# Two mixture layers on one core: the experts' output bias added on GpSimd from a table on all partitions instead of by a selector matmul

## What is computed

```python
h = gelu(einsum('bsh,bhi->bsi', x, Wi[e]) + bi[e])     # 256 -> 1024
o = einsum('bsi,bih->bsh', h, Wo[e]) + bo[e]           # 1024 -> 256, bo: 8 x 256
r = o + x
y = (r - mean(r)) * rsqrt(var(r) + 1e-12) * gamma[e] + beta[e]
```

## Time and profile before

| | before |
|---|---|
| median of 3 runs | 488.36 us (488.33 to 488.38) |
| profiled execution | 488.29 us |
| its span, first to last instruction | 486.5 us |
| mean granted TensorE clock | 0.98 |
| busy: PE, DVE, ACT, POOL | 458.1, 341.8, 362.3, 343.7 us |

### The profile page before, as it was taken

One profiled execution on the slowest core, in us unless ns is written; L12 is line 12 of the kernel. 1 busy time (PEld: TensorE's weight loads), 2 busy tenths in 40 slices (PEclk: granted clock), 3 DMA queues, 4 the chain that ended last, 5 costly groups with the idle time before them and its releaser, 6 DMA issues.

```text
span 486.5 us, 18826 instructions
## 1 busy us (share of the span) xinstructions
PE 458.1 (94%) x5724; PEld 423.3 (87%) x5725; DVE 341.8 (70%) x910; ACT 362.3 (74%) x1087; POOL 343.7 (71%) x567
## 2 busy tenths in 40 slices
PE   3599999999999999999999999999999999999972
PEld 2388999999999999999999999999999999888861
DVE  7677777777777777777777787777777766665352
ACT  2499777887777877778877788777787777776631
POOL 5043677887778877887778877887778877754565
PEclk9889999999999999999999999999999999999995
DMA  3924334333333343433433333333332222220001
GB/s 105 333 73 106 95 99 104 104 102 92 98 100 95 103 104 87 99 96 102 104 89 95 102 101 98 86 98 101 101 98 65 60 62 61 62 56 25 26 22 34
DMA packets 66806, 44.33 MB, mean 91 GB/s; under 512 B 41537, under 2 KB 58322, under 8 KB 66642
## 3 DMA queue, kind: packets, MB, share of 16 engines
q1 hardware_dynamic: 65744, 43.68, 33.4%
q10 hardware_dynamic: 1026, 0.21, 0.2%
HBM read 35.47 MB, written 8.39 MB: 90 GB/s over the span
## 4 chain that ended last, share of the span: by engine, by line
PE 89%; DVE 3%; issue 2%; POOL 2%; ACT 2%; DMA 0%; POOLq 0%; DVEq 0%
PE p_o L1019 12%; PE p_o L1017 12%; PE p_o L1018 12%; PE p_h L1006 12%; PE p_h L1008 11%; PE p_h L1007 11%; PE p_d L1029 7%; PE p_u L1043 6%; PE p_t L1051 3%; PE p_u L1039 2%; PE p_o L1117 1%; PE p_h L947 1%; DVE W L810 1%; ACT h L639 0%; ACT ctab L591 0%
## 5 line engine op out<-in xcount | busy, mean ns | idle before, releaser
L1006 PE MATMUL p_h<-x_hi,W 128*128 128x128 f16 (+1 forms) x1088 | 183.5, 217 | 3.3 <-issue 3.3
L1007 PE MATMUL p_h<-x_lo,W 128*128 128x128 f16 (+1 forms) x1088 | 183.3, 217 | 0.0
L1008 PE MATMUL p_h<-x_hi,W 128*128 128x128 f16 (+1 forms) x1088 | 183.3, 217 | 0.0
L639 ACT ACTIVATE h<-p_h,bi_tile 128x128 f32<-128x128 f32 (+1 forms) x544 | 149.0, 359 | 0.0
L1018 PE MATMUL p_o<-W,h_hi 128*128 x512 | 139.6, 273 | 0.0
L1017 PE MATMUL p_o<-W,h_hi 128*128 x512 | 139.6, 273 | 0.0
L1019 PE MATMUL p_o<-W,h_lo 128*128 x512 | 139.5, 273 | 0.0
L1006 PEld LDWEIGHTS p_h<-x_hi,W 128*128 x1088 | 105.7, 98 | 9.3 <-issue 8.0
L1007 PEld LDWEIGHTS p_h<-x_lo,W 128*128 x1088 | 105.7, 98 | 1.9
L1008 PEld LDWEIGHTS p_h<-x_hi,W 128*128 x1088 | 105.6, 98 | 0.0
L539 POOL TENSOR_TENSOR rs<-mv,neg_half 128x1 f32<-128x1 f32 x64 | 55.1, 861 | 69.7 <-DVE mv L882 69.7
(11 more groups left out here) (167 smaller groups left out, 825.5 us busy)
## 6 DMA issues: line engine op xcount, KB each, us to landing
stage<-in_w SPq DMA_DIRECT2D x56, 256.0 KB, 2.7
x_nat<-in_x SPq DMA_DIRECT2D x128, 64.0 KB, 2.1
out<-y SPq DMA_DIRECT2D x128, 64.0 KB, 2.0
x_T<-in_xT SPq DMA_DIRECT2D x126, 64.0 KB, 2.2
W<-in_w SPq DMA_DIRECT2D x8, 256.0 KB, 4.8
g_t<-in_gamma SPq DMA_DIRECT2D x1, 1024.0 KB, 7.0
W<-in_expert_W SPq DMA_DIRECT2D x2, 128.0 KB, 3.0
upT<-in_up_W SPq DMA_DIRECT2D x2, 64.0 KB, 2.6
```

The source lines that it names most:

```text
L639: ins = nc.scalar.activation(h[:, c, mine], p_h[parity][:, c, mine], ACT.Gelu, bias=bi_tile[:, parity, n, c:c + 1], scale=1.0 / (XS * WS))
L1006: mm(out, hi, x_hi[:, parity, k, mine], start=(k == 0), stop=False)
L1007: mm(out, hi, x_lo[:, parity, k, mine], start=False, stop=False)
L1008: ins = mm(out, lo, x_hi[:, parity, k, mine], start=False, stop=(k == KD - 1))
```

## The change

`bo` is loaded onto all 128 partitions as a table `bo_t` of 8 x 256 float32 (1 MB in all, 8 KB a partition), from SP's queue just ahead of `g_t`. In step i POOL adds the row of the expert of tile i-1 to `x_nat` of that tile in place, between L535 and L539, once the tile's samples have been loaded. For a mixed tile it does so by halves. DVE's L859 waits for this (`xb_done`) instead of for the load. L1117 goes, and the first matmul of the second product opens the sum. The preparation of `bo_parts` goes on all engines.

```diff
+        bo_t = sb("bo_t", [P, E0 * D])
-        bo_parts = sb("bo_parts", [P, D], f16)
...
+            sp.dma_start(bo_t[:, :], t["bo"].partition_broadcast(P)).then_inc(bo_in, 16)
             sp.dma_start(g_t[:, :], t["gamma"].partition_broadcast(P)).then_inc(g_in, 16)
...
-            link(pool.memset(bo_parts[:, :], 0.0))
...
-            pool.wait_ge(b_ready, 1)
-            split_rows(b_s[:, :], b_rest, b_16, bo_parts)
-            pool.sem_inc(bo_ready, 1)
...
+                if exists(i - 1):
+                    pool.wait_ge(xnat_in[1 - parity], loads(i - 1, 1 - parity, 2))
+                    if isinstance(i, int) and i == 1:
+                        pool.wait_ge(bo_in, 16)
+                    if mixed(i - 1):
...
+                    else:
+                        pool.tensor_tensor(x_nat[:, 1 - parity, :], x_nat[:, 1 - parity, :],
+                                           bo_t[:, bass.ds(e_last * D, D)], ALU.add).then_inc(xb_done, 1)
...
-            act.dma_start(bo_rows, t["bo"].rearrange("(e d) -> e d", d=D)).then_inc(bo_in, 16)
...
-            act.wait_ge(b_summed, 1)
-            nc.scalar.copy(b_s[:, :], ph_flat[0][:, 0:D]).then_inc(b_ready, 1)
...
-                if isinstance(i, int) and i == 0:
-                    dve.wait_ge(bo_ready, 1)
...
-                    dve.wait_ge(xnat_in[parity], loads(i - 2, parity, 2))
+                    dve.wait_ge(xb_done, i - 1)
...
-            mm(ph_flat[0][:, 0:D], sel9[0:E0, :, :].rearrange("p a b -> p (a b)"), bo_rows, start=True, stop=True)\
-                .then_inc(b_summed, 1)
...
-                    mm(p_o[:, 0:D], h_high[at], hi, start=False, stop=False)
+                    mm(p_o[:, 0:D], h_high[at], hi, start=(j == 0 and n == 0), stop=False)
...
-                    pe.wait_ge(sel_done, i)
-                    if isinstance(i, int) and i == 1:
-                        pe.wait_ge(bo_ready, 1)
-                    mm(p_o[:, 0:D], sel_tile[:, (four + 3) % 4, :], bo_parts[:, :], start=True, stop=False)
```

More of the change, by code:

```diff
@@ L144, in build @@
         part_16 = home(0, E0 - 2).bitcast(f16)
-        bo_rows, b_s, b_rest = y[0:E0, 0, :], z1, yT[:, :, :].rearrange("p k t -> p (k t)")
-        b_16 = h_lo[:, 0, :, :].rearrange("p c q -> p (c q)")
         tok_i = sb("tok_i", [P, 2], i32)
@@ L211, in build @@
         u_ready = sem("u_ready")
-        b_summed = sem("b_summed")
-        b_ready = sem("b_ready")
-        bo_ready = sem("bo_ready")
+        xb_half = sem("xb_half")
+        xb_done = sem("xb_done")
         parts_ready = sem("parts_ready")
@@ L503, in step @@
             def step(i, parity, four, weights):
-                e_third, e_before, _, _, e_next = indices(pool, i + (IDX_EXP - 3), 5, E0 - 1)
+                e_third, e_before, e_last, _, e_next = indices(pool, i + (IDX_EXP - 3), 5, E0 - 1)
                 if exists(i - 5):
@@ L535, in step @@
                     pool.tensor_tensor(rs[:, 0:1], mv[:, 0, 1:2], neg_half[:, 0:1], ALU.pow).then_inc(rs1_done, 1)
+                if exists(i - 1):
[3 more added lines that the diff above has]
+                    if mixed(i - 1):
+                        first_e, second_e = experts(i - 1, e_last)
+                        pool.tensor_tensor(x_nat[HALF[0], 1 - parity, :], x_nat[HALF[0], 1 - parity, :],
+                                           bo_t[HALF[0], bass.ds(first_e * D, D)], ALU.add).then_inc(xb_half, 1)
+                        pool.wait_ge(xb_half, i - PURE)
+                        pool.tensor_tensor(x_nat[HALF[1], 1 - parity, :], x_nat[HALF[1], 1 - parity, :],
+                                           bo_t[HALF[1], bass.ds(second_e * D, D)], ALU.add).then_inc(xb_done, 1)
+                        pool.wait_ge(xb_done, i)
+                    else:
+                        pool.tensor_tensor(x_nat[:, 1 - parity, :], x_nat[:, 1 - parity, :],
+                                           bo_t[:, bass.ds(e_last * D, D)], ALU.add).then_inc(xb_done, 1)
                 if exists(i - 4):
@@ L931, in _ @@
             ins.then_inc(turned, 1)
-            pe.wait_ge(pool_step, 3)
-            pe.wait_ge(bo_in, 16)
-            mm(ph_flat[0][:, 0:D], sel9[0:E0, :, :].rearrange("p a b -> p (a b)"), bo_rows, start=True, stop=True)\
-                .then_inc(b_summed, 1)
             pe.wait_ge(slots_ready, 1)
@@ L964, in _ @@
             pe.wait_ge(embb_ready, 1)
-            pe.wait_ge(pool_step, 8)
+            pe.wait_ge(pool_step, 7)
             pe.wait_ge(rows_in, 2 * 16)
```

## The result

The changed kernel takes 491.94 us (median of 5 runs, 491.42 to 493.64) against 488.33 us before (5 runs, 488.26 to 488.38). The ratio is 1.0079, with a 95% interval of 1.0068 to 1.0090: slower by 0.8%, where 482.7 us was forecast. The profiled execution is the slowest of the five, 493.64 us with a span of 491.8. Its differences are told against the execution profiled before (488.29 us): 5.35 us more.

A forecast was written before the change was run, and what follows sets the result against it. The prediction took PE, gapless in the main stretch, to bound the kernel. It summed 488.29 - 6.76 (matmuls) + 0.2 (mixed tiles) + 1.0 (head) = 482.7 us, with a range of 481.0 to 486.0.

The forecast's parts named there:

- What bounds the kernel, and the matmul's price: Main stretch: PE has no gap, so each L1117 removed saves 0.109 us; 6.76 us for 62 of them.
- GpSimd's queue has room: POOL between L535 and L539: the add fits in a wait of 1.03 us, cost zero.
- Where the add meets DVE: Each step: add delays L879 by some 0.25 us, then L882 and z1; taken as zero, bounds zero and 2.5 us.
- the circle of 6.80 us: POOL and DVE: L879, L539, L535 and the add's letting go in turn, 6.80 us against a wished step of 6.56.
- Their slack is 0.67 - 0.11 = 0.56 us: Room of z1 before PE's transposes need it; the largest delay, 0.5 us, was held to be just under it.
- in the third the add would come behind L879's wish: Third step of the delay on DVE: the add comes later than L879 and the delay falls back to nothing.
- The first rival: Slower: the lock between add and L879 decides every step if z1's slack is under about 0.37 us; about 494.3 us, chance 0.08.
- The head: First steps: POOL's add and `parts` come late, first power near 40.5 us; +1.0 us taken, between 0 and 2.
- The end: Mixed steps: two adds of half the partitions leave more than a microsecond before the same power on average; cost zero.
- The 1 MB table and the loads: SP's queue: the table's transfer is hidden, at zero; x_nat's loads have 2.4 us of cover in the steady state, cost zero.

The follow-up runs named there:

- no_add: Changed kernel with GpSimd's adds left out, waits and semaphores kept (output bias missing): 481.55 us, ratio 0.9858 to the kernel before.
- two_powers: Changed kernel with two 128x1 powers on GpSimd in place of the add (bias missing): 484.46 us, ratio 0.9913 to the kernel before.
- parts_first: Changed kernel with the preparation of `parts` moved ahead of all else in POOL's step 1: 491.06 us, ratio 1.0059 to the kernel before.
- add_early: Changed kernel with the add moved ahead of the gamma product (L522) in GpSimd's step: 484.75 us, ratio 0.9919 to the kernel before.
- turn_later: Changed kernel with PE's transposes of z1 one block of the second product later (TR_AT 5 instead of 4): 491.80 us, ratio 1.0068.
- add_192_columns: Changed kernel with the pure tiles' add cut from 256 to 192 columns (64 columns lack their bias): 484.93 us, ratio 0.9929.
- index_ahead: Changed kernel, PE's loop unrolled 8 steps, with the next step's indices loaded ahead of PE's wait for z1: 486.46 us, ratio 0.9962.
- parts_and_early: Changed kernel with `parts` prepared first in POOL's step 1 and the add ahead of the gamma product in every step: 483.01 us, ratio 0.9883.
- after_unroll8: Changed kernel with PE's loop unrolled 8 steps instead of 4: 491.09 us, ratio 1.0043 to the kernel before.

## Why the prediction was wrong

- **What bounds the kernel, and the matmul's price: right.** 0.11 us a step was measured where nothing else stood in the way (main 342.1 to 336.5 us in `no_add`).
- **GpSimd's queue has room: right, and of no use.** The wait of L548 fell from 69.7 to 29.2 us, near the 20 to 30 forecast, and `two_powers` fills that wait fully without loss.
- **Where the add meets DVE: the mechanism was right, the room was wrong.** The delay of about 0.25 us, its growth by as much in the next step and the circle of 6.80 us came as worked out: L882 at 0.58 and 0.81, adds 6.80 us apart. The step that failed is "Their slack is 0.67 - 0.11 = 0.56 us". That is the distance from the end of `z1` to the transposes. PE never starts them sooner than 0.06 us behind `z1`, so even there only 0.5 was free. And `z1` has to be in time for more: about 1.68 us must lie between its end and the next first product, 2.2 at a loop head. Before, 2.2 lay there in an ordinary step; less 0.11 and less 1.68 leaves 0.41, and at a loop head (2.3 there, less 0.11) nothing. L882's delay reaches 0.52 in the circle's later steps, which is just over the one and well over the other. So "in the third the add would come behind L879's wish" failed with it: PE yielded, and the wish moved along with the add. At 11 of the 12 heads of the main stretch the delay of `z1` is paid in full, in steps of 7.25 instead of 6.75. I had taken zero, with 2.5 us as the bound; it is 8.2 us in the profiled execution (344.7 less the 336.5 of `no_add`). The term was mis-sized by looking for the reader of `z1` and not for what else waits behind the same wait.
- **The first rival: near, and too small a chance.** It said that the circle becomes the step if the room is under about 0.37 us, and gave it 0.08. The room is 0.41 and zero at the heads, so it happened in part: two or three steps of four keep 6.56, and the rest pays. Its 494.3 us was closer than the forecast. The Trainium skill ("SBUF — State Buffer", section "Who interferes with whom") states for this an exclusive lock between VectorE and GpSimd, held for the whole instruction. The trace agrees in that L882 is held until near the add's end whenever the add started first. It differs in two points: L882 ends 0.15 us behind the add though it takes 0.29, so the hold ends some 0.14 us ahead of the add's recorded end; and a power of 128x1, which reads SBUF too, didn't hold L882 at all (`two_powers`). The rival was named, and priced by the wrong room. The prediction also read the earlier trace rows as two operations holding each other up. The row ahead of them on DVE says what held the first:

```profile
40.95 0.68 DVE L810 SCALAR_TENSOR_TENSOR W<-stage,W 128x512 f16<-128x512 f32 x1
```

L530 was held until near the end of L810 (41.63), and L843 then until near the end of L530 (42.21): one after the other, not both at once.
- **The head: the mechanism right, the size short by the clock.** POOL's first power came at 40.55 us, where 40.5 had been worked out. First transposes 42.00 against 40.75 us, +1.25 where +1.0 was taken and 0 to 2 given. That 0.3 of it would be `z1` held by the add was not seen: the prediction looked for such a meeting with L879 only. DVE's sorting got shorter as forecast: the instruction that had taken 0.52 us took 0.17. The wait on PE, 2.34 us against "some 2", was there too; that the granted clock would then fall for 1.6 us more was not in the sum.
- **The end: missed.** The mixed tiles' two adds were priced at zero. Beside the last of them (POOL's adds, then DVE):

```profile
470.55 0.99 POOL L536 TENSOR_TENSOR x_nat<-x_nat,bo_t 64x256 f32<-64x256 f32 x1
471.73 0.72 POOL L539 TENSOR_TENSOR x_nat<-x_nat,bo_t 64x256 f32<-64x256 f32 x1 [0.18 <-POOL x_nat L536]
```

```profile
470.59 1.24 DVE L848 SCALAR_TENSOR_TENSOR h_lo<-h,h_hi 128x256 f16<-128x256 f32 x2
471.75 0.85 DVE L893 TENSOR_SCALAR z<-r,mv,rs 128x256 f32<-128x256 f32 x1
```

L893 took 0.85 us for 0.41 again and ended 0.15 us behind the add, though it reads one tensor only. So `z1` itself was held, and L1048 at 472.66 us waited 0.73 for it. The end lost 0.73 us in after and 0.9 in `parts_first`, and nothing in `no_add` and `add_early`, nor in `turn_later`, where the transposes come later.
- **The 1 MB table and the loads: right.** POOL waits for `x_nat` once only in after, 16.8 us at the head, where it has nothing else to do until then but `parts`.

## What to carry to other kernels

A GpSimd operation that fits in a wait of GpSimd's queue isn't free yet: look at which DVE operations want to start while it runs. Here those with two inputs in SBUF were held (L882, L848), and so was a `tensor_scalar` with one (L893); the batch-norm statistics (0.43 us) and the operations with one input in PSUM (L862 and L871, 0.42 us) took the same time beside it as alone, and beside them it belongs. The room of a late result is not only the distance to its reader on PE but also that to the next point where PE's stream must be ahead, and at loop heads there was none. A place in the order 3 us away was worth 7 us here, as much as the matmul that the change took out.

## What the runs showed of the hardware

- PE needs 1.67 us from the end of `z1` to the next step's first matmul here, and about 2.2 us at a loop head, whether the transposes stand at the 5th or the 6th block; with the index loads ahead of the wait it started after 1.63 without a gap.
- A power of 128x1 on GpSimd, 0.55 us long, didn't delay a two-input DVE operation beside it (0.29 us). An add of 128x256 (0.73 us) that had started first held it until some 0.14 us before the add's recorded end (up to 0.89 us).
- A `tensor_scalar` of 128x256 float32 on DVE, with one SBUF input, was held too: 0.80 and 0.85 us for 0.41 in after, 0.81 in `parts_first`, and 0.67 beside the shorter add of `add_192_columns` (0.59). Batch-norm statistics (0.43) and operations with one input in PSUM (0.42) were not, in some 50 steps each.
- The granted clock fell at the head in the profiled executions with PE waits of 2.34 (after), 2.34, 2.55 and 2.81 us there (`index_ahead`, `two_powers`, `add_early`; mean 0.83 from 40 to 50 us in each), and stayed at 1.00 in four with 1.72 to 2.27 us (`parts_and_early`, `turn_later`, `add_192_columns`, `after_unroll8`). Where it fell, the first gelu came 4.8 to 5.0 us behind the first transposes instead of 3.3. No run changed this wait and nothing else.
- What stays open: how often the clock falls in executions that were not profiled, and so how the 3.6 us of the medians divide between head and main stretch; and what PE's stream does in the 1.67 us.
